# Gated local and global attention: its last four stages made one by chunks, with the next attention's spectral filter folded into its weights in between

## What is computed

```python
# L3a, last steps (x is the normed input)
diff = local_m - glob_m
gate_h = silu(concatenate([x, diff], -1) @ Wg.T + bg)
alpha = sigmoid(gate_h @ Wgo.T + bgo)
mixed = alpha * local_m + (1.0 - alpha) * glob_m
return mixed @ Wo.T + bo

# L3b, the filter (D_HEAD = 8, so 5 frequencies)
mask = sigmoid(mask_logits)
q = irfft(rfft(q) * mask); k = irfft(rfft(k) * mask)
```

## Time and profile before

| what | value |
|---|---|
| median of 3 runs | 5073.88 us (5073.15 to 5074.03) |
| profiled execution, its own time | 5081.62 us |
| its span in the trace | 5079.5 us |
| TensorE, VectorE, ScalarE, GpSimd busy | 88%, 64%, 52%, 18% of the span |
| TensorE's granted clock, mean of the span | 0.92 of full speed |
| from the first transpose of global_out to the next norm's first matmul | 3726.61 to 3750.38 us |
| from the experts' last copy to the first matmul of L3b's norm | 4023.26 to 4030.95 us |

### The profile page before, as it was taken

The page is one execution under the profiler, slowest core; times in us unless marked ns, Lnnn a source line. Parts: engine busy times, 40 slices in busy tenths (PEclk is TensorE's granted clock), DMA queues, the critical chain, the costliest instruction groups (busy, mean ns, idle before and its releaser), DMA issues. The chain is left out here.

```text
span 5079.5 us, 65564 instructions
## 1 busy us (share of the span) xinstructions
...
## 2 busy tenths in 40 slices
...
GB/s 64 21 58 42 39 37 21 17 17 0 8 1 3 5 3 5 5 11 60 20 27 27 27 17 2 66 56 1 1 9 17 15 67 26 26 26 26 3 21 21
DMA packets 43961, 116.67 MB, mean 23 GB/s; under 512 B 14359, under 2 KB 15503, under 8 KB 42895
## 3 DMA queue, kind: packets, MB, share of 16 engines
...
...
## 5 line engine op out<-in xcount | busy, mean ns | idle before, releaser
L1218 DVE TENSOR_REDUCE 34_heads_mx<-34_heads_mps 128x1 f32<-128x1024 f32 x512 | 604.0, 1220 | 69.5 <-PE 34_heads_mps L1070 68.4
L1218 DVE TENSOR_REDUCE 57_heads_mx<-57_heads_mps 128x1 f32<-128x1024 f32 x512 | 604.0, 1220 | 68.6 <-PE 57_heads_mps L1070 67.6
L1188 ACT ACTIVATE 57_heads_p<-57_heads_sps 128x512 f32<-128x512 f32 x1024 | 552.8, 596 | 114.0 <-PE 57_heads_sps L1095 110.3
L1188 ACT ACTIVATE 34_heads_p<-34_heads_sps 128x512 f32<-128x512 f32 x1024 | 552.7, 596 | 114.0 <-PE 34_heads_sps L1095 110.0
L2218 ACT ACTIVATE 24_latent_heads_p<-24_latent_heads_ring 128x512 f32<-128x512 f32 x512 | 277.2, 595 | 378.9 <-PE 24_latent_heads_ring L2137 378.9
L1218 DVE TENSOR_REDUCE 8_heads_mx<-8_heads_mps 128x1 f32<-128x1024 f32 (+7 forms) x384 | 333.8, 908 | 161.5 <-PE 8_heads_mps L1078 108.2
L2241 DVE TENSOR_REDUCE 24_latent_heads_mx<-24_latent_heads_ring 128x1 f32<-128x512 f32 x512 | 323.1, 685 | 170.0 <-PE 24_latent_heads_ring L2117 170.0
L1188 ACT ACTIVATE 8_heads_p<-8_heads_sps 128x512 f32<-128x512 f32 (+3 forms) x640 | 307.2, 533 | 174.6 <-PE 8_heads_sps L1098 149.0
L1095 PE MATMUL 34_heads_sps<-32_head_rows_qs,32_head_rows_ks 123*128 123x512 bf16 x1024 | 311.2, 386 | 8.0 <-ACT 34_heads_p L1188 4.9
L1095 PE MATMUL 57_heads_sps<-53_head_rows_qs,53_head_rows_ks 123*128 123x512 bf16 x1024 | 311.3, 386 | 7.8 <-ACT 57_heads_p L1188 4.9
L2133 PE MATMUL 24_latent_heads_ring<-24_latent_heads_qc,20_mla_mem_keys 64*128 64x512 f32 x1024 | 272.8, 610 | 3.3 <-DMA 21_mla_loop_mem_mrow<-24_latent_heads_mT 3.3
...
## 6 DMA issues: line engine op xcount, KB each, us to landing
...
```

Of the source, the lines that this page charges most:

```text
L1188: act.activation(pslot[x % PS][:, 0:CW - off], sps[e % SB][:, 0:CW - off], ACT.Exp, scale=SCALE / 2).then_inc(ex_done, 1)
L1218: dve.tensor_reduce(mx[h % 2][:, i, half:half + 1], mps[x % 2][:, 0:w], AX.X, ALU.max).then_inc(mx_taken, 1)
```

## The change

The four stages become one, `gated_sum`. It keeps the work of the four, chunk by chunk: TensorE transposes all four chunks, then makes the four hidden chunks in two banks by turns (each waits for the silu of the chunk two before), then the filter's two products into a bank that the transposes have left, then the four gate chunks in two banks by turns. ScalarE makes the filter's mask first of all, then the four copies, the four silus and the four sigmoids. VectorE makes the four differences, then the filter's five terms and its two copies, then the mix, as two steps for each chunk. SP loads the basis at the start. The two copies overwrite the projection weights of L3b (`L3b_wq`, `L3b_wk`) in place; they are read nowhere else. The stage "filter" goes from `filtered_attention`, and the function `project` goes.

```diff
--- before.py
+++ after.py
@@ -477,57 +477,6 @@
                     sp.wait_ge(g.out_done, 16 * NC)
 
 
-def project(g, name, jobs, weights):
-
-    nc = g.nc
-    NB = 8
...
-
 def first_attention(g):
 
 
@@ -1293,45 +1243,8 @@
         with ExitStack() as inner:
             qT = inner.enter_context(nc.sbuf_tensor("L3b_qT", [P, T], F32))
             kT = inner.enter_context(nc.sbuf_tensor("L3b_kT", [P, T], F32))
-            with Stage(g, "filter") as st:
-                basis, filt, mask = st.sb("basis", [P, N_FREQ, P]), st.sb("filt", [P, P]), st.sb("mask", [P, N_FREQ])
-
-                filtered = [st.sb(f"filtered_{n}", [P, P]) for n in "qk"]
-                basis_in, mask_ready, done, multiplied, kept = (st.sem(n) for n in ("basis_in", "mask_ready", "done", "multiplied", "kept"))
-                with Stage(g, "filter_product") as product:
-                    ps = product.ps("ps", [P, 2, P])
-                    with nc.Block() as block:
...
-                        @block.tensor
-                        def _(pe):
-                            pe.wait_ge(ready, 16)
-                            pe.wait_ge(done, N_FREQ)
-                            for i, n in enumerate(("L3b_wq", "L3b_wk")):
-                                ins = pe.matmul(ps[:, i, :], W[n], filt[:], start=True, stop=True)
-                            ins.then_inc(multiplied, 1)
-
-                        @block.vector
-                        def _(dve):
-                            ch = Chain(dve, done)
-                            dve.wait_ge(basis_in, 16)
-                            dve.wait_ge(mask_ready, 1)
-                            ch.link(dve.tensor_scalar(filt[:], basis[:, 0, :], mask[:, 0:1], None, ALU.mult))
-                            for f in range(1, N_FREQ):
-                                ch.link(dve.scalar_tensor_tensor(filt[:], basis[:, f, :], mask[:, f:f + 1], filt[:],
-                                                                 ALU.mult, ALU.add))
-                            dve.wait_ge(multiplied, 1)
-                            for i in range(2):
-                                dve.tensor_copy(filtered[i][:], ps[:, i, :]).then_inc(kept, 1)
-                residual_and_norm(g, *g.pending, jobs_ready=ready, heads=Heads(rows, (qT, kT), [
-                    Job(qT, [(filtered[0][:], g.nT)]), Job(kT, [(filtered[1][:], g.nT)])], Vt, W["L3b_wv"]))
+            residual_and_norm(g, *g.pending, jobs_ready=ready, heads=Heads(rows, (qT, kT), [
+                Job(qT, [(W["L3b_wq"], g.nT)]), Job(kT, [(W["L3b_wk"], g.nT)])], Vt, W["L3b_wv"]))
         attnT = mem.enter_context(nc.sbuf_tensor("L3b_attnT", [P, T], F32))
         head_loop(g, Vt, attnT, rows, causal=False)
         residual_and_norm(g, [(attnT, W["L3b_wout"])], W["L3b_bout"], router=(W["L3f_Wr"], W["L3f_br"], g.loaded["L3f"]))
@@ -2903,31 +2816,91 @@
                     add_level(G)
 
 
-def global_channels(g, glob_tok, local, glob, diff):
-
-    nc = g.nc
-    with Stage(g, "global_out") as st:
+def gated_sum(g, glob_tok, local, glob, diff, hidden, alpha):
+
+
+    nc, nT, W, ready = g.nc, g.nT, g.W, g.loaded["L3a"]
+    with Stage(g, "gated") as st:
         back = [st.ps(f"back{c}", [P, CW]) for c in range(NC)]
-        turned, copied, taken = st.sem("turned"), st.sem("copied"), st.sem("taken")
+        hps = [st.ps(f"hps{i}", [P, CW]) for i in range(2)]
+        gps = [st.ps(f"gps{i}", [P, CW]) for i in range(2)]
+        basis, filt, mask = st.sb("basis", [P, N_FREQ, P]), st.sb("filt", [P, P]), st.sb("mask", [P, N_FREQ])
+        weights = [W["L3b_wq"], W["L3b_wk"]]
+        turned, copied, taken, h_ready, h_done, gate_ready, gate_done, mixed = (st.sem(n) for n in (
+            "turned", "copied", "taken", "h_ready", "h_done", "gate_ready", "gate_done", "mixed"))
+        basis_in, mask_ready, filt_done, multiplied, kept = (st.sem(n) for n in ("basis_in", "mask_ready", "filt_done", "multiplied", "kept"))
         with nc.Block() as block:
+            @block.sync
+            def _(sp):
+                sp.dma_start(basis[:], g.big["filter_basis"].rearrange("p (f q) -> p f q", q=P)).then_inc(basis_in, 16)
+
             @block.tensor
             def _(pe):
-                for c in range(NC):
+                def back_chunk(c):
                     for i in range(TPC):
                         ins = pe.transpose(back[c][:, tile(i)], glob_tok[:, tile(TPC * c + i)], g.ident[:])
                     ins.then_inc(turned, 1)
 
+                def hide(c):
+                    if c >= 2:
+                        pe.wait_ge(h_done, c - 1)
+                    pe.matmul(hps[c % 2][:], W["L3a_Wg"][:, 0:P], nT[:, chunk(c)], start=True, stop=False)
+                    pe.wait_ge(taken, c + 1)
+                    pe.matmul(hps[c % 2][:], W["L3a_Wg"][:, P:2 * P], diff[:, chunk(c)], start=False, stop=True).then_inc(h_ready, 1)
+
+                def gate(c):
+                    pe.wait_ge(h_done, c + 1)
+                    if c >= 2:
+                        pe.wait_ge(gate_done, c - 1)
+                    pe.matmul(gps[c % 2][:], W["L3a_Wgo"], hidden[:, chunk(c)], start=True, stop=True).then_inc(gate_ready, 1)
+
+                for c in range(NC):
+                    back_chunk(c)
+                pe.wait_ge(ready, 16)
+                for c in range(NC):
+                    hide(c)
+                pe.wait_ge(g.loaded["L3b"], 16)
+                pe.wait_ge(filt_done, N_FREQ)
+                for i in range(2):
+                    ins = pe.matmul(back[0][:, tile(i)], weights[i], filt[:], start=True, stop=True)
+                ins.then_inc(multiplied, 1)
+                for c in range(NC):
+                    gate(c)
+
             @block.scalar
             def _(act):
+                act.wait_ge(g.loaded["L3b"], 16)
+                act.activation(mask[:], W["L3b_mask"], ACT.Sigmoid).then_inc(mask_ready, 1)
                 for c in range(NC):
                     act.wait_ge(turned, c + 1)
                     act.activation(glob[:, chunk(c)], back[c][:], ACT.Identity).then_inc(copied, 1)
+                act.wait_ge(ready, 16)
+                for c in range(NC):
+                    act.wait_ge(h_ready, c + 1)
+                    act.activation(hidden[:, chunk(c)], hps[c % 2][:], ACT.Silu, bias=W["L3a_bg"]).then_inc(h_done, 1)
+                for c in range(NC):
+                    act.wait_ge(gate_ready, c + 1)
+                    act.activation(alpha[:, chunk(c)], gps[c % 2][:], ACT.Sigmoid, bias=W["L3a_bgo"]).then_inc(gate_done, 1)
 
             @block.vector
             def _(dve):
                 for c in range(NC):
                     dve.wait_ge(copied, c + 1)
                     dve.tensor_tensor(diff[:, chunk(c)], local[:, chunk(c)], back[c][:], ALU.subtract).then_inc(taken, 1)
+                ch = Chain(dve, filt_done)
+                dve.wait_ge(basis_in, 16)
+                dve.wait_ge(mask_ready, 1)
+                ch.link(dve.tensor_scalar(filt[:], basis[:, 0, :], mask[:, 0:1], None, ALU.mult))
+                for f in range(1, N_FREQ):
+                    ch.link(dve.scalar_tensor_tensor(filt[:], basis[:, f, :], mask[:, f:f + 1], filt[:], ALU.mult, ALU.add))
+                dve.wait_ge(multiplied, 1)
+                for i in range(2):
+                    dve.tensor_copy(weights[i], back[0][:, tile(i)]).then_inc(kept, 1)
+                mix = Chain(dve, mixed)
+                for c in range(NC):
+                    dve.wait_ge(gate_done, c + 1)
+                    mix.link(dve.tensor_tensor(diff[:, chunk(c)], diff[:, chunk(c)], alpha[:, chunk(c)], ALU.mult))
+                    dve.tensor_tensor(diff[:, chunk(c)], diff[:, chunk(c)], glob[:, chunk(c)], ALU.add)
 
 
 def hale_attention(g):
@@ -2974,17 +2947,7 @@
             global_inputs(g, qp, qtok, ntok, Wc, w)
             linear_levels(g, qp, qtok, ntok, Wc, tri, means, own_head, fixed_in, glob_tok)
             glob, hidden, alpha = ntok, qp, qtok
-            global_channels(g, glob_tok, local, glob, kl)
-            project(g, "gate_hidden", [Job(hidden, [(W["L3a_Wg"][:, 0:P], nT), (W["L3a_Wg"][:, P:2 * P], kl)], W["L3a_bg"], ACT.Silu)], ready)
-            project(g, "gate", [Job(alpha, [(W["L3a_Wgo"], hidden)], W["L3a_bgo"], ACT.Sigmoid)], ready)
-            with Stage(g, "mix") as mx:
-                done = mx.sem("done")
-                with nc.Block() as block:
-                    @block.vector
-                    def _(dve):
-                        ch = Chain(dve, done)
-                        ch.link(dve.tensor_tensor(kl[:], kl[:], alpha[:], ALU.mult))
-                        ch.link(dve.tensor_tensor(kl[:], kl[:], glob[:], ALU.add))
+            gated_sum(g, glob_tok, local, glob, kl, hidden, alpha)
             residual_and_norm(g, [(kl, W["L3a_Wo"])], W["L3a_bo"], router=(W["L3f_Wr"], W["L3f_br"], g.loaded["L3f"]))
```

50 lines of the change are left out of this document (removed).

## The result

The changed kernel takes 5063.82 us (median of 12 runs, 5059.48 to 5066.77); the kernel before, on the same chip, 5073.95 (12 runs, 5070.82 to 5079.47). The ratio is 0.9979, with a 95% interval of 0.9970 to 0.9988: 10.1 us less, between 6.1 and 15.2. The forecast was 5062.9. Run again on another chip as an experiment, the same kernel gave 13.8 us less (ratio 0.9974, 0.9965 to 0.9984).

The account below looks back on a forecast made before the run. No engine bounds the gated stretch; the order of its steps does, and at the filter every engine stops. Savings of 4.1 + 6.9 = 11.0 us from the median 5073.88 give 5062.9 us, range 5060.0 to 5068.0.

Parts of the forecast that it names:

- The removed filter stage: Before L3b's norm: the norm starts 0.80 us after the experts' last copy, with no filter between; 6.9 us saved.
- The moved filter: In the merged gated stage: the filter's DMA, mask, five VectorE steps, products and copies are hidden; cost nothing.
- The edge of the cover: In the merged stage: a basis landing over 9.2 us after its issue delays the gates, microsecond for microsecond.
- The four stages as one: First transpose to next norm's first matmul: merged stage starts that norm at 3746.29 instead of 3750.38; 4.1 us saved.
- The ring of two banks: Hidden matmuls: with only two banks, chunk 2 waits for silu 0; price 0.65 us.
- The boundary: From the mix's end to the next norm's first matmul: 0.32 us, against 0.52 behind the wide step.
- Sigmoid's load behind the gate: Rival at the gates: sigmoid's table load follows the gate wait, later steps 0.7 us later; gain 10.3, chance 0.10.
- The cold start lasts: Rival in the merged stage: TensorE's clock stays low through hidden and gate matmuls; net gain 2.8 us, chance 0.06.
- Half of the cold start: Rival in the merged stage: half the lasting low clock, so only the filter pays; 5067.0 us, chance 0.07.
- The drain of the tables: Rival at silu and sigmoid: each table load brings a second wait of its length; gain 8.4 us, chance 0.04.
- The experts lose their clock: Rival in the experts behind the earlier norm: TensorE's clock granted below 0.95, costing over 11 us; chance 0.03.
- More from a hot start of the norms: Rival at both norms: full clock at their start saves 0.45 and 0.9 us more; 5061.5 us, within forecast's own range.

Follow-up runs that it names:

- the halves alone: Kernel before with only the four stages merged, 5068.2 us (ratio 0.9985); with only the filter's work spread over the four stages, 5066.77 us (0.9983).
- the version that is covered: Changed kernel with the filter's basis asked for only once the fourth difference is taken: 5063.57 us.
- the one that pays: Changed kernel with the filter's basis asked for only once three hidden chunks are made: 5067.36 us.
- the two kernels with a wide and a linked last step: Changed kernel with the mix as two steps over all 2048 columns, 5065.86 us; with VectorE waiting for its own last mix step, 5062.71 us.
- the version with TensorE's sum: Against a version using sigmoid times argument for silu, gates between hidden chunks: mix's addition moved into the next norm's projection; 5058.55 us, 0.9969 of the kernel before.
- the version with silu's load ahead: Changed kernel with ScalarE's wait for the L3a weights moved to the head of its list, leaving one wait before the first silu: 5064.62 us.
- three later profiles: Two of the changed kernel with silu made from sigmoid and gates between hidden chunks (5065.13, 5060.81 us), one with the mix in whole-row steps (5065.86 us).

## Why the prediction was right

**The sum.** Forecast 4.1 + 6.9 = 11.0; the profile of after shows 4.4 + 6.9 = 11.3, and the halves alone 4.3 and 6.9. The medians gave 10.1 on one chip and 13.8 on another; with intervals some 9 us wide it is luck that the first came so near to the forecast. The stretches carry the account. The chance of 0.66 that the prediction gave to a gain over 0.2% is not settled by a ratio of 0.9979 with 0.998 inside its interval.

**The removed filter stage, 6.9.** As forecast, and for the reason given: the norm starts 0.80 behind the copies in every kernel without the stage.

**The moved filter, nothing.** Shown from two sides. The first copy came 1.37 us behind the first transpose where 1.39 was put; the products 10.7 behind it, where 11.0 was put, with no wait. The edge of the cover was put at a basis that lands 9.2 us behind the first transpose: VectorE had it at 7.9 in the version that is covered, and at 12.8 in the one that pays. The prediction priced what lies beyond the edge at a microsecond each; the clock that falls in the wait made it dearer in the one execution, 4.2 us for products 3.5 us late.

**The four stages as one, 4.1.** Step by step against the profile, counted from the first transpose, forecast then measured: silu load 5.5, 5.2; sigmoid load 11.9, 11.6; first sigmoid 13.2, 12.9; norm 19.7, 19.4. The whole 0.3 us comes in at the start: the hidden matmuls began 3.20 us behind the first transpose instead of 3.42, and their first step took 0.86 instead of 0.94, both because the clock rose sooner. Behind that no step is off by more than a few hundredths. The ring of two banks cost the 0.65 that it was put at (0.66 in the profile, 0.67 by the experiment), though TensorE's idle time ahead of the third chunk reads 0.40 and not 0.65, since the tail of the last pass counts as busy and the rest is a slower restart; the load ahead of the single wait is where the prediction put it and is worth 0.65; and a chunk of the mix takes 1.33 for 1.34.

**The step that failed by its reason.** The boundary was forecast at 0.32 with the words that it is 0.52 "behind the wide step". It measured 0.30, but the width is not the cause, as the two kernels with a wide and a linked last step show: it is VectorE's wait for its own last step. The number was right because the reference, the filter's copies, are unlinked too.

**What was taken as fixed and is not.** The prediction put the rise of TensorE's clock at 3.5 us behind the first transpose, from one profile. Over the fourteen profiled executions it came between some 3 and 6 us, and G moves with it by up to 0.6 us in one and the same stage (19.36 and 19.87 for the changed kernel, and 19.98 for the one with the linked step, less its 0.24). And the prediction read the three runs of 5073.15 to 5074.03 as the spread of the kernel; the 12 runs of before span 8.6 us. That the forecast lay only a microsecond beyond what can be told from no change was so, and two measurements of the same kernel fell on 10.1 and 13.8.

**The rivals.** *Sigmoid's load behind the gate*: not so, and priced at 0.65 by the experiment. *The cold start lasts*: not in the changed kernel; in the version with TensorE's sum, where the clock rose latest, it cost one microsecond of a chunk, not the four that the rival put down for the whole stage. *Half of the cold start*: not so, the gate stages gave their 4.4. *The drain of the tables*: the first sigmoid starts 0.02 us behind its load (3733.99 + 1.28, then 3735.29), and the mask and the silu follow theirs as closely (3722.31 + 1.28, then 3723.61; 3727.52 + 1.28, then 3728.81); in the version with silu's load ahead the silu started 0.17 later, and waited for its matmul. The Trainium skill (ScalarE: Activation LUTs, What ACT_TABLE_LOAD costs) adds some 1380 ns of drain to every switch; the trace doesn't agree. The prediction's use of that rule had a slip besides: the kernel before makes the same two switches on its path, so a cost of each would be in both kernels and would leave the gain where it is. *The experts lose their clock*: not here, the stage is 236.6 us long in both. But the argument against it, that the stage holds 1.00 once it is busy, is not what the rows show: its first 12 us had 0.72 in both kernels, and in three later profiles 0.57, with a stage 1.7 us longer. So the rival is real in a small size, and that the changed kernel met the same clock there as the kernel before was not foretold. *More from a hot start of the norms*: the first norm's eight matmuls did take 1.46 instead of 2.05 us, and VectorE's first statistics began 0.5 us sooner behind the norm's start; its last came no sooner, 11.39 us behind that start against 11.32. VectorE ends that stage. The second norm's first matmuls took 1.08 us, as before.
